# One block of window attention and routed experts on one core: v projected by 32x32 tiles beside q and k, router logits with tokens on the partitions

## The chip, the cores and the metric

The kernel runs on one core of one Trainium2 chip. The metric is the device time in microseconds (us), the median of the runs shown. TensorE is called PE, VectorE DVE, ScalarE ACT, GpSimd POOL and SyncE SP, as in the profile.

## What is computed

The input x is 8 images of 64 channels and 96 x 96 pixels, in fp32. A layer norm over the channels comes first, then attention in windows of 4 x 4 pixels, 8 heads, over each half of the channels, once plain and once rolled by two pixels, with a depthwise 3 x 3 convolution of v added. Then every pixel is a token for a mixture of 8 experts, of which the router picks two:

```python
qkv = jnp.einsum('oi,bihw->bohw', qkv_w, xh)
q, k, v = jnp.split(qkv, 3, axis=1)
lepe = jax.lax.conv_general_dilated(v, lepe_w, (1, 1), 'SAME', feature_group_count=c)
...
attn = jnp.einsum('nhqc,nhkc->nhqk', q * scale, k) + bias[None]
attn = jax.nn.softmax(attn, axis=-1)
out = jnp.einsum('nhqk,nhkc->nhqc', attn, v) + lepe
...
router_probs = jax.nn.softmax(x @ router_w + router_b, axis=-1)
top_p, top_i = jax.lax.top_k(router_probs, K)
expert_out = jnp.einsum('bnd,edc->bnec', x, expert_w) + expert_b
...
x = x + _L0_conv_ref(_ln_c(x), L0_conv_qkv_w, L0_conv_lepe_w, L0_conv_bias_table)
t = _to_tokens(x)
t = t + _L0_ffn_ref(_ln_t(t), L0_ffn_router_w, L0_ffn_router_b, L0_ffn_expert_w, L0_ffn_expert_b)
```

## The kernel before

Everything is one software pipeline, written out by hand. Its step is a **slot**: one unit of eight windows. Three units make a strip (4 image rows, 384 pixels) and two strips, six slots, make a tile. There are 576 units, 192 strips and 96 tiles. `LAG` says how many slots behind the start each stage works, and `pipeline()` calls every engine's `slot()` for each slot number: 72 slots written out, then a hardware loop of 72 slots (12 tiles, one image) that runs six times, then the rest written out. Each engine goes through its own instructions in the order of its `slot()`, and only semaphores tie the engines together, so an engine may be ahead of another by a slot or more. Below, "slot 0" to "slot 5" are slot numbers modulo six.

The channels and the plain and rolled copies fill the 128 partitions in four groups of 32. What PE does, by line of the kernel:

- every slot: **score** (L632, 32 matmuls of 32x32 with 64 columns, on top of a bias that ACT has placed in the bank) and **product** (L717, 32 matmuls with 32 columns of weights and 16 moving columns; in slots 1 and 4 also L723, the sums of the softmax, four matmuls into `bank_d`). In slots 2 and 5 the product begins a strip and waits for `fin_made` of the strip before, since both use `bank_o`.
- slots 2 and 5: **value** (L657), one 128x128 matmul with 384 columns. Slots 0 and 3: **q and k** (L670, L671), eight matmuls of 32x32 with 384 columns, each group of rows taking q to its own group of columns and k to the one two further on.
- by tile: **centre** (L731, slot 0), **variance** (L648, slot 1), the convolution in three steps (L697, slots 4, 5 and 0), **tile_sum** (L737, slot 3, needs `bank_p[1]` back from the k of the same slot), **tile_variance** (L742, slot 4), the expert bias (L756, slot 4), **turn_gates** (L640, slot 5), **router** (L748, slot 5), the turned logits (L681, slot 2), and the four expert pairs (L617), in slots 0, 1, 1 and 2.

The fp32 matmuls appear twice in the trace, as two passes of PE, so that the 32 matmuls of a score are 64 records.

ACT, in a slot: the softmax sums (L781, L783) after slots 1 and 4, v (L802), exp (L806), the bias for the score two units on (L812), q twice (L820), k (L829), and the norm's pieces (L841, L842 after tile_sum). DVE, in a slot: row maximum (L956) and subtraction (L961) of the last score, `y_out` (L970, needs the last expert pair), `fin` (L976, needs L783), the turned v (L984), `yn` (L995), the logits (L999), y in three steps (L991, L1005, L1011), the turned probabilities (L1019, needed by the product one slot later), and between them 17 small steps that choose the experts. POOL issues the DMAs that spread k and v (L573, L585) and pair `yn` (L595).

An expert pair's place in the slot is given by a table: place 0 is behind the score, place 1 behind q and k.

```python
EXPERT_AT = {(0, 0): 0, (1, 0): 1, (1, 1): 2, (2, 0): 3}
```

## Time and profile before

| | |
|---|---|
| median of 3 runs | 3418.93 us (3413.72 to 3419.05) |
| the profiled execution, its own time | 3416.38 us |
| its span, first to last instruction | 3414.6 us |
| busy: PE, DVE, ACT, POOL | 3076.2 us (90%), 2233.1 us (65%), 1619.7 us (47%), 2509.8 us (74%) |
| chain that ended last | PE 81%, issue 8%, DVE 5%, ACT 4% |
| granted PE clock, mean | 0.942 of full speed |
| instruction queue q8 | 688 packets, 11.27 MB |
| PE instructions | 84772 matmul records and as many weight loads |

A busy PE is not PE at its peak, since the ends of pipelined matmuls are modelled. What one group of matmuls costs is therefore read from its start to the start of the next group, not from its duration. The time in brackets behind a row is how long the engine stood idle ahead of it and for whom; "issue" is idle time in which it waited for nothing that the profile shows.

### The profile page before, as it was taken

The page shows a single profiled execution, that of the slowest core. Times are in us where ns is not written, and L with a number is a line of the kernel's source. Part 1 is how long each engine was busy: PE and PEld are TensorE (multiplying, and loading weights), DVE is VectorE, ACT ScalarE, POOL GpSimd, SP SyncE. Part 2 cuts the span into 40 slices and gives each one's busy share as a digit, 9 for nine tenths or more (in the row PEclk, how much of TensorE's full clock was granted, in tenths as well). Part 3 has the DMA queues.
Part 4 walks back from the last instruction along what each step waited for, and adds up shares of the span by engine and source line. Part 5 has one row for each costly group of instructions (what it writes and reads, how often), then busy time and mean ns, then how long its engine had stood idle before and what let it go on. Part 6 is the DMA issues. An engine that isn't in the chain of part 4 may idle for free.

```text
span 3414.6 us, 201082 instructions
## 1 busy us (share of the span) xinstructions
PE 3076.2 (90%) x84772; PEld 1798.8 (53%) x84772; DVE 2233.1 (65%) x4807; ACT 1619.7 (47%) x3362; POOL 2509.8 (74%) x4998
## 2 busy tenths in 40 slices
PE   4899999989989899998999989999899999999987
PEld 2555555545555455554555545555455555555553
DVE  2566767656666666666666757666666666666666
ACT  2554545445444454444444445444454444444441
POOL 4887777767777677777777767777677777777771
PEclk7999999999999999999999999999999999999998
DMA  2456665656565565556565656666565656565656
GB/s 64 105 138 160 159 160 155 160 131 168 148 167 149 145 165 147 155 153 153 150 168 147 163 139 158 161 155 166 133 170 148 168 152 163 152 162 146 163 138 178
DMA packets 436964, 517.64 MB, mean 152 GB/s; under 512 B 116400, under 2 KB 405168, under 8 KB 435888
## 3 DMA queue, kind: packets, MB, share of 16 engines
q1 hardware_dynamic: 270128, 390.67, 42.8%
q0 software_dynamic: 165888, 113.57, 13.9%
q8 instruction: 688, 11.27, 1.5%
q14 instruction: 260, 2.13, 0.2%
HBM read 312.67 MB, written 77.86 MB: 114 GB/s over the span
## 4 chain that ended last, share of the span: by engine, by line
PE 81%; issue 8%; DVE 5%; ACT 4%; DMA 1%; DVEq 0%; POOL 0%; SPq 0%; ACTq 0%; POOLq 0%
PE bank L632 18%; PE bank L717 14%; PE bank L697 13%; PE bank L617 9%; PE bank L723 4%; PE bank L657 3%; PE bank L670 3%; PE bank L737 3%; PE bank L742 2%; PE bank L731 2%; PE bank L756 2%; PE bank L648 2%; PE bank L748 2%; ACT qx L820 2%; ACT bank L812 1%
## 5 line engine op out<-in xcount | busy, mean ns | idle before, releaser
L585 POOL DMA_DIRECT2D vx<-vt x3072 | 1562.1, 517 | 443.6 <-PE bank L723 433.8
L573 POOL DMA_DIRECT2D kx<-k_sb x1536 | 739.2, 489 | 386.7 <-issue 241.7
L717 PEld LDWEIGHTS bank<-probT,vx 128*32 128x32 f32 x36864 | 605.5, 150 | 445.9 <-issue 387.8
L717 PE MATMUL bank<-probT,vx 128*32 128x16 f32 x36864 | 668.0, 210 | 146.9 <-issue 132.7
L632 PEld LDWEIGHTS bank<-kx,qx 32*32 32x32 f32 x36864 | 598.1, 112 | 345.4 <-issue 332.4
L632 PE MATMUL bank<-kx,qx 32*32 32x64 f32 x36864 | 700.7, 226 | 76.6 <-issue 54.2
L949 DVE TENSOR_TENSOR gx<-gate_wide,yn_pair 128x768 f32<-128x768 f32 x384 | 365.6, 953 | 384.5 <-PE bank L617 380.4
L697 PE MATMUL bank<-halo,conv_w 128*64 128x380 f32 (+6 forms) x2592 | 479.5, 497 | 0.1
L806 ACT ACTIVATE prob<-prob 128x512 f32<-128x512 f32 x576 | 360.0, 625 | 244.4 <-DVE prob L961 222.3
L961 DVE TENSOR_TENSOR prob<-bank,row_max 128x512 f32<-128x512 f32 x576 | 398.5, 692 | 16.7
L956 DVE TENSOR_REDUCE row_max<-bank 128x32 f32<-128x512 f32 x576 | 382.8, 665 | 37.8 <-PE bank L632 33.2
L1019 DVE STREAM_TRANSPOSE probT<-prob 128x512 f32<-128x512 f32 x576 | 405.1, 703 | 0.3
L976 DVE TENSOR_TENSOR fin<-bank,row_inv 128x384 f32<-128x384 f32 x192 | 106.2, 553 | 408.4 <-ACT row_inv L783 408.0
L617 PE MATMUL bank<-gx,table 128*64 128x384 f32 x1536 | 341.9, 525 | 5.8 <-DVE gx L949 4.2
L812 ACT ACTIVATE bank<-bias_tile 128x512 f32<-128x512 f32 x576 | 339.5, 589 | 0.0
L697 PEld LDWEIGHTS bank<-halo,conv_w 128*64 128x64 f32 x2592 | 180.9, 149 | 245.9 <-issue 236.7
L820 ACT ACTIVATE qx<-bank,table 128x384 f32<-128x384 f32 x384 | 200.6, 573 | 151.8 <-PE bank L670 151.7
L846 ACT ACTIVATE yrstd<-bank,table 128x384 f32<-128x384 f32 x96 | 55.8, 581 | 394.0 <-PE bank L742 394.0
L595 POOL DMA_DIRECT2D yn_pair<-yn x384 | 201.3, 531 | 51.4 <-DVE gx L949 33.8
L802 ACT ACTIVATE v_sb<-bank 128x384 f32<-128x384 f32 x192 | 94.4, 492 | 210.1 <-PE bank L657 209.6
L670 PE MATMUL bank<-xs,table 32*32 32x384 f32 x1536 | 180.1, 509 | 11.1 <-issue 9.8
L657 PE MATMUL bank<-xs,table 128*128 128x384 f32 x384 | 172.0, 530 | 19.6 <-DMA xs<-xn 19.6
(72 smaller groups left out, 2959.9 us busy)
## 6 DMA issues: line engine op xcount, KB each, us to landing
gate_wide<-gate_rows SPq DMA_DIRECT2D x768, 192.0 KB, 3.9
vx<-vt POOLq DMA_DIRECT2D x3072, 12.0 KB
halo<-xn SPq DMA_DIRECT2D x160, 240.0 KB
kx<-k_sb POOLq DMA_DIRECT2D x1536, 24.0 KB
z<-fin SPq DMA_DIRECT2D x192, 192.0 KB
yn_pair<-yn POOLq DMA_DIRECT2D x384, 96.0 KB, 3.2
xa<-in_x SPq DMA_DIRECT2D x96, 192.0 KB, 3.1
xn<-xa SPq DMA_DIRECT2D x192, 96.0 KB, 2.5
```

What stands on the lines that cost most here:

```text
L573: pool.dma_start(kx[to + m:to + C:4, r % 2, m, :], k_sb[at + m:at + C:4, r % 2, :])\
L585: pool.dma_start(vx[to:to + TOK, r % 2, col:col + 25:8, odd, :], vt[at:at + TOK, r % 2, x::2, :, :].rearrange("p h n k -> p h (n k)"))\
L617: last = MM(bank_f[half * C:(half + 1) * C, 0:SPX], const("experts")[:, p * C:(p + 1) * C], gx[:, p % 2, half, :], start=False, stop=(p == ...
L632: last = MM(bank_s[r % 2][at, w * KEYS:(w + 1) * KEYS], qx[at, kr % 2, win, :, :].rearrange("p a i -> p (a i)"), kx[at, kr % 2, :, win * T ...
L697: last = MM(by_rows(bank_c[half * C:(half + 1) * C, 0:SPX])[:, top:end, low:high], conv_w[:, which, group * 3 + side, :], by_rows(halo[:, ...
L717: last = MM(bank_o[32 * c:32 * c + 32, at * TOK:(at + 1) * TOK], vx[:, kr % 2, :, at % 2, at // 2 * 4 + ba], probT[:, kr % 2, at, ba * TOK ...
L806: S.activation(prob[:, r % 4, :], prob[:, r % 4, :], ACT.Exp).then_inc(exp_made, 1)
L812: S.activation(bank_s[r % 2][:, :], bias_tile[:, :, :].rearrange("p n k -> p (n k)"), ACT.Copy).then_inc(bias_placed, 1)
L949: V.tensor_tensor(gx[:, p % 2, :, :], gate_wide[:, p, :, :], yn_pair[:, r % 2, :, :], ALU.mult)\
L956: V.tensor_reduce(row_max[:, r % 2, :], per_row(bank_s[r % 2][:, :]), AX.X, ALU.max).then_inc(max_made, 1)
L961: V.tensor_tensor(per_row(prob[:, r % 4, :]), per_row(bank_s[r % 2][:, :]), over_keys(row_max[:, r % 2, :]), ALU.subtract).then_inc(shifte ...
L1019: V.transpose(probT[:, kr % 2, j * UW:(j + 1) * UW, :].rearrange("p n k -> p (n k)"), prob[:, r % 4, :]).then_inc(probT_made, 1)
```

## The change

Five things are done to the order and the shape of the work:

1. **v beside q and k.** The value matmul of slots 2 and 5 goes. In slots 0 and 3 each group of rows now makes three 32x32 matmuls, q to its own group of columns, v to the next and k to the one after; v goes to `bank_d`, the bank of the softmax sums, so the group waits for `log_made` and the sums wait for `v_copied`.
2. **Logits with tokens on the partitions.** The router's 128x16 matmul with 384 columns, ACT's copy of it (L852) and the three transposes in slot 2 (L681) go. Twelve matmuls with 32 tokens of `yn` as weights and the router's 16 columns moving take their place in slot 5; DVE adds the router's bias when it takes the logits, at the head of slot 0.
3. **Behind the product.** The convolution's steps of slots 5 and 0, and the expert pairs of place 1, stand behind the product; the last pair moves from slot 2 place 0 to slot 2 place 1.
4. **ACT** copies k first, then q twice, then v, all in slots 0 and 3.
5. **DVE** makes `y_out` at the end of slot 2 and no longer near its head.

```diff
-EXPERT_AT = {(0, 0): 0, (1, 0): 1, (1, 1): 2, (2, 0): 3}
+EXPERT_AT = {(0, 0): 0, (1, 0): 1, (1, 1): 2, (2, 1): 3}
...
                 if st := s.strip("query_key"):
                     k, r = st
                     if (s.n - LAG["router"] - 1) % TSLOT == 0 and (ti := Slot(s.n - 1, s.turn).tile("router")):
+                        pe.wait_ge(fln_made, ti[0] + 1)
+                        pe.wait_ge(logit_saved, ti[0] + 1)
+                    if s.later(r, 4):
+                        pe.wait_ge(log_made, k - 3)
...
+                    wait_alone(pe, xs_loaded[r // 2 % 2], (k // 4 + 1) * (XS_DMAS * 16))
                     for g in range(4):
+                        at, to_v, to_k = (slice((g + n) % 4 * CH, (g + n) % 4 * CH + CH) for n in range(3))
                         q_last = MM(bank_p[0][at, 0:SPX], wq[at, at], xs[at, r % 4, :], start=True, stop=True)
+                        k_last = MM(bank_p[1][to_k, 0:SPX], wk[at, at], xs[at, r % 4, :], start=True, stop=True)
+                        v_last = MM(bank_d[to_v, 0:SPX], wv[at, at], xs[at, r % 4, :], start=True, stop=True)
...
                     if j == UNITS - 1:
+                        pe.wait_ge(v_copied, strips_to(s, k + 4))
...
+                expert(1)
+                conv((1, 2))
...
-                    MM(bank_p[1][0:GE, 0:SPX], const("router"), yn[:, r % 2, :], start=True, stop=True)\
-                        .then_inc(logitT_made, 1)
+                    for blk in range(TBLK):
+                        for c in range(4):
+                            last = MM(bank_p[1][32 * c:32 * c + 32, blk * GE:(blk + 1) * GE],
+                                      yn[:, r % 2, blk * 128 + 32 * c:blk * 128 + 32 * c + 32], const("router"),
+                                      start=True, stop=True)
+                    last.then_inc(logit_made, 1)
```

On PE, from the variance of slot 1 to the product of slot 2, the order before was this (`gx` belongs to the expert pairs, `kx,qx` to the score, `probT,vx` to the product, `probT,table` to the softmax sums, `xs` to value, `logitT` to the turned logits):

```order
L648 MATMUL bank<-sq,table 128x384 [waits k_saved,sq_made]
...
L617 MATMUL bank<-gx,table 64x384 [waits gx_made]
L617 MATMUL bank<-gx,table 64x384
L717 MATMUL bank<-probT,vx 32x16 [waits probT_made]
L717 MATMUL bank<-probT,vx 32x16 x31
L723 MATMUL bank<-probT,table 32x384 x4
...
L632 MATMUL bank<-kx,qx 32x64 x31
...
L617 MATMUL bank<-gx,table 64x384
...
L657 MATMUL bank<-xs,table 128x384 [waits sq_made]
L681 MATMUL bank<-table,logitT 128x16 [waits ln_made,logitT_saved]
...
L717 MATMUL bank<-probT,vx 32x16 [waits log_made,fin_made,v_spread0]
```

And in the same place of the changed kernel (L672 is the variance, L707 the product, L714 the sums, L656 the score):

```order
L672 MATMUL bank<-sq,table 128x384 [waits k_saved,sq_made]
L707 MATMUL bank<-probT,vx 32x16 [waits probT_made]
L707 MATMUL bank<-probT,vx 32x16 x31
...
L714 MATMUL bank<-probT,table 32x384 [waits v_copied]
L714 MATMUL bank<-probT,table 32x384 x3
...
L617 MATMUL bank<-gx,table 64x384 [waits gx_made]
L617 MATMUL bank<-gx,table 64x384
...
L656 MATMUL bank<-kx,qx 32x64 x31
...
L707 MATMUL bank<-probT,vx 32x16 [waits log_made,fin_made,v_spread0]
```

The sums stand ahead of an expert pair, value and the turned logits are gone, and the product of slot 2 follows its score directly.

On ACT, slot 3 with what stands around it, before (from the placed bias of slot 2 to the norm after tile_sum):

```order
L812 ACTIVATE bank<-bias_tile 128x512 [waits shifted]
L806 ACTIVATE prob<-prob 128x512 [waits shifted]
L812 ACTIVATE bank<-bias_tile 128x512 [waits shifted]
L820 ACTIVATE qx<-bank,table 128x24x16 [waits q_made,score_made]
L820 ACTIVATE qx<-bank,table 128x24x16
L829 ACTIVATE k_sb<-bank 128x384 [waits k_spread1,k_made]
L841 ACTIVATE yn<-bank 128x384 [waits yn_paired1,fc_made]
```

The same place after the change:

```order
L803 ACTIVATE bank<-bias_tile 128x512 [waits shifted]
L797 ACTIVATE prob<-prob 128x512 [waits shifted]
L803 ACTIVATE bank<-bias_tile 128x512 [waits shifted]
L811 ACTIVATE k_sb<-bank 128x384 [waits k_spread1,k_made]
L819 ACTIVATE qx<-bank,table 128x24x16 [waits q_made,score_made]
L819 ACTIVATE qx<-bank,table 128x24x16
L827 ACTIVATE v_sb<-bank 128x384 [waits vt_made,v_made]
L838 ACTIVATE yn<-bank 128x384 [waits yn_paired1,fc_made]
```

The copy of k is now the first of four copies, and v the last.

On DVE, slot 2, before (with the row maximum of slot 2 at its head):

```order
L956 TENSOR_REDUCE row_max<-bank 128x32 [waits score_made]
L961 TENSOR_TENSOR prob<-bank,row_max 128x512 [waits max_made]
...
L970 TENSOR_TENSOR y_out<-bank,y 128x384 [waits out_stored1]
...
L976 TENSOR_TENSOR fin<-bank,row_inv 128x24x4x4 [waits z_stored1]
...
L1019 STREAM_TRANSPOSE probT<-prob 128x512 [waits exp_made]
```

And after, from the subtraction of slot 2 to the row maximum of slot 3:

```order
L958 TENSOR_TENSOR prob<-bank,row_max 128x512 [waits max_made]
...
L967 TENSOR_TENSOR fin<-bank,row_inv 128x24x4x4 [waits z_stored1]
...
L1006 STREAM_TRANSPOSE probT<-prob 128x512 [waits exp_made]
...
L1019 TENSOR_TENSOR y_out<-bank,y 128x384 [waits out_stored1]
...
L953 TENSOR_REDUCE row_max<-bank 128x32 [waits score_made]
```

`y_out` has gone from ahead of `fin` to behind the turned probabilities.

## Rows read from the trace of the kernel before

**Rows 1.** Windows, one turn of the loop: engines busy, PE clock, DMA share, GB/s.

```profile
1264.00:1684.00 420.00, 384.40 (x10564) 224.05 (x10564) 277.40 (x595) 200.81 (x417) 311.59 (x622) 0.94 0.59 153
```

**Rows 2.** Timeline of PE: start, us, line, operation, [idle before]; slot 1 to 3.

```profile
547.94 0.91 PE L648 MATMUL bank<-sq,table 128*128 128x384 f32 x2
548.78 0.87 PE L617 MATMUL bank<-gx,table 128*64 128x384 f32 x4
549.58 1.11 PE L717 MATMUL bank<-probT,vx 128*32 128x16 f32 x64
550.52 0.83 PE L723 MATMUL bank<-probT,table 128*32 128x384 f32 x8
551.28 1.10 PE L632 MATMUL bank<-kx,qx 32*32 32x64 f32 x64
...
553.10 0.91 PE L657 MATMUL bank<-xs,table 128*128 128x384 f32 x2
...
554.43 1.11 PE L717 MATMUL bank<-probT,vx 128*32 128x16 f32 x64
...
560.44 0.91 PE L737 MATMUL bank<-y,table 128*128 128x384 f32 x2 [1.82 <-ACT k_sb L829]
```

**Rows 3.** Timeline of ACT, slots 2 and 3 of the same tile.

```profile
551.42 0.49 ACT L781 ACTIVATE row_inv<-bank 128x384 f32<-128x384 f32 x1 [0.39 <-PE bank L723]
551.95 0.52 ACT L783 ACTIVATE row_inv<-row_inv 128x384 f32<-128x384 f32 x1
...
557.92 0.63 ACT L806 ACTIVATE prob<-prob 128x512 f32<-128x512 f32 x1 [2.36 <-DVE prob L961]
...
558.98 1.03 ACT L820 ACTIVATE qx<-bank,table 128x384 f32<-128x384 f32 x2
559.90 0.49 ACT L829 ACTIVATE k_sb<-bank 128x384 f32<-128x384 f32 x1
```

**Rows 4.** Timeline of DVE, slots 2 and 3 of the same tile.

```profile
553.31 0.56 DVE L970 TENSOR_TENSOR y_out<-bank,y 128x384 f32<-128x384 f32 x1 [1.36 <-PE bank L617]
...
557.19 0.69 DVE L961 TENSOR_TENSOR prob<-bank,row_max 128x512 f32<-128x512 f32 x1
```

**Rows 5.** Timeline of PE, slots 3 to 0 of the tile before.

```profile
526.88 1.33 PE L737 MATMUL bank<-y,table 128*128 128x384 f32 x2 [1.83 <-ACT k_sb L829]
...
533.46 0.91 PE L742 MATMUL bank<-ysq,table 128*128 128x384 f32 x2
...
536.32 0.82 PE L657 MATMUL bank<-xs,table 128*128 128x384 f32 x2
537.07 1.50 PE L697 MATMUL bank<-halo,conv_w 128*64 128x380 f32 x8
...
539.44 0.80 PE L748 MATMUL bank<-yn,table 128*16 128x384 f32 x2
540.17 1.09 PE L632 MATMUL bank<-kx,qx 32*32 32x64 f32 x64
541.20 0.87 PE L617 MATMUL bank<-gx,table 128*64 128x384 f32 x4
```

**Rows 6.** Timeline of PE, q and k of slot 0: first records of both passes, next group.

```profile
542.00 0.50 PE L670 MATMUL bank<-xs,table 32*32 32x384 f32 x1
...
542.34 0.48 PE L670 MATMUL bank<-xs,table 32*32 32x384 f32 x1
...
542.80 0.54 PE L697 MATMUL bank<-halo,conv_w 128*64 128x380 f32 x2
```

**Rows 7.** Timeline of DVE, `fin` of slot 5 in that tile.

```profile
536.60 0.56 DVE L976 TENSOR_TENSOR fin<-bank,row_inv 128x384 f32<-128x384 f32 x1 [4.19 <-ACT row_inv L783]
```

**Rows 8.** Waits of PE in 1180 to 1584: for whom, us, times, longest.

```profile
PE bank L717 <- issue: 15.6, 12, 2.0
```

**Rows 9.** Timeline of PE at the loop's branch, two turns.

```profile
1167.76 0.86 PE L632 MATMUL bank<-kx,qx 32*32 32x64 f32 x47 [3.28 <-issue]
...
1589.37 0.92 PE L632 MATMUL bank<-kx,qx 32*32 32x64 f32 x25 [3.02 <-issue]
```

More of the change, by code:

```diff
@@ L619, in expert, with conv @@
                     last.then_inc(expert_made, 1)
+                def conv(sides):
+                    ti = s.in_tile("conv")
+                    if not ti or ti[2] not in sides:
+                        return
+                    k, r, side = ti
+                    t, dw = (r + 1) % IMT, SIDES[side]
+                    if side == 0:
+                        pe.wait_ge(halo_loaded[r % 2], halos_to(s, r) * 16)
+                        if s.later(r, 1):
+                            pe.wait_ge(y_step, k * 2 - 1)
+                    low, high = max(0, -dw), W - max(0, dw)
+                    first = [side == 0, side == 0]
+                    for group, skip in ((0, 0), (1, 2)):
+                        parts = [(half, *rows) for half in range(2) for rows in conv_rows(t, half)[group]]
+                        for half, top, end, which in sorted(parts, key=lambda part: part[1]):
+                            at = half * SP + skip
+                            last = MM(by_rows(bank_c[half * C:(half + 1) * C, 0:SPX])[:, top:end, low:high],
+                                      conv_w[:, which, group * 3 + side, :],
+                                      by_rows(halo[:, r % 2, :])[:, at + top:at + end, low + dw:high + dw],
+                                      start=first[half], stop=(side == 2 and group == 1), skip_group_check=True)
+                            first[half] = False
+                    if side == 2:
+                        last.then_inc(conv_made, 1)
                 if u := s.unit("score"):
@@ L796, in slot @@
                     S.activation(rstd[:, r % 2, :], rstd[:, r % 2, :], ACT.Exp, scale=-0.5).then_inc(rstd_made, 1)
-                if st := s.strip("value"):
-                    k, r = st
-                    act.wait_ge(v_made, k + 1)
-                    if s.later(r, 2):
-                        act.wait_ge(vt_made, k - 1)
-                    S.activation(by_window(v_sb[:, r % 2, :]), windows(bank_p[0][:, 0:SPX]), ACT.Copy).then_inc(v_copied, 1)
                 if u := s.unit("shift"):
@@ L815, in slot @@
                     k, r = st
+                    act.wait_ge(k_made, k + 1)
+                    if s.later(r, 2):
+                        act.wait_ge(k_spread[r % 2], k // 2 * (K_DMAS * 16))
+                    S.activation(by_window(k_sb[:, r % 2, :]), windows(bank_p[1][:, 0:SPX]),
+                                 ACT.Copy).then_inc(k_saved, 1)
+                if st := s.strip("query_key"):
+                    k, r = st
                     if s.later(r, 2):
@@ L1026, in slot @@
                 gate_work((10, 12), (0, 0))
+                if yt := s.tile("tile_out"):
+                    k, r = yt
+                    dve.wait_ge(expert_made, (k + 1) * PAIRS)
+                    if s.later(r, 2):
+                        dve.wait_ge(out_stored[r % 2], k // 2 * 16)
+                    V.tensor_tensor(y_out[:, r % 2, :], bank_f[:, 0:SPX], y[:, r % 4, :], ALU.add).then_inc(y_out_made, 1)
             pipeline(dve, slot)
```

88 lines of the change are left out of this document (19 added, 69 removed).

## Prediction, made before the changed kernel ran

> **What bounds the kernel now.** I read the busy shares first, then the windows of one turn of the loop, and then the timelines of PE, ACT and DVE over one tile. In a turn PE is busy 384.40 of 420 us, against 277.40 for DVE, 200.81 for ACT and 311.59 for POOL [rows 1], so PE sets the pace and the question is what fills its 35 us per tile (the loop's branch comes again after 1589.37 - 1167.76 = 421.6 us, which is 12 tiles) [rows 9]. The reader is to see two kinds of stretch. From the variance of slot 1 to the tile_sum of slot 3, 547.94 to 560.44, PE takes 12.50 us and stands idle 1.82 us at the end, waiting for ACT's copy of k [rows 2]. That copy is the end of a chain that starts on PE itself: expert pair, `y_out`, then DVE without a pause to the subtraction of slot 3 (553.31 to 557.88), then ACT: exp, bias, q twice, k [rows 3, 4]. From tile_sum to the next variance (526.88 to 547.94, 21.06 us) PE has no wait and is the bound by itself [rows 2, 5].
>
> Two losses lie on top. The clock granted over the turn is 0.94, which with levels of 2.4 and 1.2 GHz means 12% of the time at 1.2 GHz, so 6% of 35 us, 2.1 us a tile. And PE waits for "issue" inside the product: 15.6 us in 12 waits over 12 tiles, 1.3 us a tile [rows 1, 8].
>
> **The change, part by part.** All of it is summed against the profiled execution, span 3414.6 and time 3416.4 us; the median of the runs is 2.5 us above that, which I leave out.
>
> *Value, slot 5.* Its 128x128 matmul goes: 537.07 - 536.32 = 0.75 us from start to start [rows 5]. *Value and turned logits, slot 2:* 554.43 - 553.10 = 1.33 us [rows 2]. *v beside q and k.* q and k, sixteen records, take 542.80 - 542.00 = 0.80 us, of which the two passes are 0.34 us apart and the eight records of a pass start within 0.04 us [rows 6]. No row shows three groups of rows writing into one group of columns. The bounds: 0.03 us if four more tiles start beside the others (two passes of four records at that spacing), 0.68 us (two passes of 0.34) if v goes in passes of its own, and up to 8 x 0.34 = 2.7 us if its tiles queue one behind another. I take 0.03, since the nearest row, the softmax sums, has four matmuls stream different data through the same rows at once: eight records of 384 columns in 551.28 - 550.52 = 0.76 us, where one after another at 0.34 us they would take 2.7 us [rows 2, 6]. Below nothing is excluded, since work is only added there.
>
> That the four q tiles, which lie in different groups of rows and share one PSUM bank, start together is what the same sixteen records show. The Trainium skill (TensorEngine Tiling, Gotcha 1: PSUM Pressure) says the opposite, that different row tiles cannot use the same bank at the same time; by that rule q and k would take 2.7 us or more, and v would add as much again. The trace does not agree at 0.80 us, so the rule stays a rival only.
>
> *Router, slot 5.* The old matmul takes 540.17 - 539.44 = 0.73 us [rows 5]. The new one is 24 records of the product's form, whose 64 take 550.52 - 549.58 = 0.94 us [rows 2]: 24/64 of it, 0.35 us. Bounds: 0.2 (a quarter of the product's time) and 0.73 as before. Saved: 0.38 us. ACT loses a copy, which was never late; DVE's logits become an addition of the same size.
>
> *Moves of the expert pairs and the convolution.* They change nothing in PE's sum. What they change is who waits. The products of slots 2 and 5 wait for `fin`, and now come sooner after what `fin` depends on.
>
> *Slot 5.* `fin` starts 536.60 - 533.46 = 3.14 us after tile_variance and lasts 0.56 [rows 5, 7]; nothing in the change makes it earlier. The product would come where value stood, 536.32 - 533.46 = 2.86 us after it. It starts at 3.14 + 0.56 + 0.1 = 3.8: a **new wait** of 0.95 us, where the old order had value and the convolution in front. Behind the waiting product stand the convolution, the router and the next score; all slip by it. The bounds are nothing and 1.4 us (if v_copied or the turned v holds DVE up).
>
> *Slots 1 to 3.* Count from the variance, 0. The sums come ahead of an expert pair (0.80 us, 549.58 - 548.78 [rows 2]), but ACT is busy until its 0.39 us of idle time [rows 3], so L783 ends 552.47 - 0.39 = 552.08, at 4.14, and `fin` runs from 4.2 to 4.75. PE reaches the product of slot 2 at 0.84 + 0.94 + 0.76 + 0.80 + 1.03 = 4.37 (a score is 541.20 - 540.17 = 1.03 [rows 2, 5]) and waits 0.4 us. `y_out` no longer stands first and waits for nobody; DVE's run from `y_out` to the end of the subtraction was 557.88 - 553.31 = 4.57 us [rows 4] and holds the same operations in another order, less 0.1 us for the logits. So the subtraction of slot 3 ends at 4.2 + 4.5 = 8.7. ACT adds exp and bias, 558.98 - 557.92 = 1.06 us, and then k, 0.49 us, where q twice (559.90 - 558.98 = 0.92 us) used to come between [rows 3]. k is there at 10.3. PE by itself is done at 4.8 + 0.94 + 0.80 + 1.03 + 0.83 + 0.94 = 9.35 and waits about 0.95 us. tile_sum starts at 10.3 where it started at 12.50: 2.2 us saved.
>
> *Tile_sum to variance:* - 0.75 - 0.38 + 0.95 + 0.03 = 0.15 us saved.
>
> *Queues.* ACT's copy of v in slots 0 and 3 is last of four and delays the norm's copies after tile_sum by some 0.4 us; tile_variance comes three groups later (over 3 us), which covers it. DVE now takes the logits at the head of slot 0, so its slot 0 cannot start before PE's router is done; behind that wait stand the row maximum and two products for the experts, which PE needs only after its own score and expert pair of slot 0 (1.83 us) or later. POOL has the same DMAs; at 311.59 busy of a shorter 385 us it is at 81%, not the bound. `y_out` is stored about 1.5 us later and SP's loads of the next strips behind it are due three slots on. These I cost at nothing; if POOL's cover were gone, the spread of v would hold the product of slots 2 and 5.
>
> **Sum.** 2.2 + 0.15 = 2.35 us a tile, times 96 = 226 us: 3416 - 226 = 3190. Then the losses on top. PE's idle time at the end of slot 3 falls from 1.8 to about 0.95 us, and the slow clock stands behind that idle time; if a third of the 2.1 us goes, 0.7 us a tile comes back. Against it, the issue waits were partly hidden under the wait for k and are now barer: I give back 0.5 us. Net 0.2 us a tile, 20 us. **Forecast: 3170 us**, 7% faster, by itself 3085 to 3255 (the ends are the losses 0.9 us a tile better or worse).
>
> **The rivals.**
>
> *The clock stays up.* With idle stretches halved, the falls behind slot 3 vanish: 1.5 of the 2.1 us a tile come back instead of 0.7, and the issue waits cost nothing more: 1.3 x 96 = 125 us less, 3045 to 3065. For it: the slow stretch follows the 1.83 us wait (a tile_sum of 1.33 us there against 0.91 [rows 2, 5]). Against it: new waits in slots 2 and 5.
>
> *v in passes of its own:* 0.65 x 192 = 125 us more, 3295. For it: nothing was seen with three groups of rows into one of columns. Against it: the sums' row above.
>
> *Instruction supply.* A matmul is four records with its weight loads. A tile has six more for v (24 records) and, for the router, 48 new records less 4 and less the 6 of the three transposes: 62 more on (84772 x 2)/96 = 1766, 3.5%, and slots 2 to 4 are packed tighter. The issue waits (1.3 us a tile [rows 8]) are the sign of it. If they double in a stretch that used to be padded by waits, 1.3 - 0.5 = 0.8 us a tile, 77 us, and the clock stays as it is, 67 more: 3315. The Trainium skill (Advanced Engine Details and Errata, ISA Cache) states that instructions come in lines of 256; then a tile is 7 lines before and 7.1 after, and the positions of the waits would drift.
>
> *Slower: the tiles of v queue.* If each of v's eight passes has to follow another in its bank or its columns, the group grows by 2.7 us, 192 x 2.7 = 518 us: 3190 + 518 = 3710. It decides from 226/192 = 1.2 us a strip on. For it is the rule of the skill above; against it are q and k and the sums.
>
> *No change:* the wait for `fin` in both slots is so long that the gain is gone (over 2.35 us more a tile). It would need `fin` 2 us later than rows 7 put it.
>
> **How the numbers follow.** Forecast 0.66; clock stays up 0.08; v in passes of its own 0.09; instruction supply 0.11; v queues 0.04; no change 0.02. The likeliest is 3170. The range 3060 to 3300 holds the forecast, the clock case in part, and v in its own passes, and leaves out some 2 in 10: the tails and the slower cases. A measurement of this kernel can tell about 0.2% from no change. Faster by over 0.2%: 0.94; within: 0.02; slower: 0.04.
>
> **What would show it.** In the profile after, q, k and v: 24 records that start within 0.5 us, next group 0.8 to 0.9 us after the first. The product of slot 5 with about 0.9 us of idle time for `fin`, that of slot 2 with 0.4. tile_sum 10.3 us behind the variance, with about 1 us of idle time for k, and 19 to 21 us from there to the next variance. A router of 24 records in under 0.5 us. A granted clock over 0.95. I would be wrong if the group of q, k and v takes over 1.5 us, if the wait for k at tile_sum is still 1.8 us, or if "issue" grows to over 3 us a tile.

## The result, and the profile after

The changed kernel takes 3379.01 us (median of 12 runs, 3361.2 to 3398.93), the kernel before 3413.59 us on the same chips (12 runs). The ratio is 0.9909, 95% interval 0.9884 to 0.9935: 0.9% faster, where 7% was forecast, and outside the stated range. The profiled run took 3377.19 us, its span is 3374.9 us, its granted clock 0.958 (0.942 before).

First one of the two shortest full tiles of the changed kernel (30.5 us each), in the timeline of PE. It is called the **clean** tile below, since little is late in it. (Columns as in [rows 2]; L672 is the variance, L707 the product, L714 the sums, L656 the score, L730 tile_sum, L735 tile_variance.)

```profile
1499.59 0.91 PE L735 MATMUL bank<-ysq,table 128*128 128x384 f32 x2
...
1503.39 1.14 PE L707 MATMUL bank<-probT,vx 128*32 128x16 f32 x64 [0.78 <-issue]
1504.47 1.50 PE L637 MATMUL bank<-halo,conv_w 128*64 128x380 f32 x8
1505.89 0.38 PE L743 MATMUL bank<-table,yn 128*32 128x16 f32 x24
1506.21 0.86 PE L656 MATMUL bank<-kx,qx 32*32 32x64 f32 x47
1507.54 0.43 PE L656 MATMUL bank<-kx,qx 32*32 32x64 f32 x17 [0.47 <-issue]
...
1514.66 0.91 PE L672 MATMUL bank<-sq,table 128*128 128x384 f32 x2
1515.51 1.11 PE L707 MATMUL bank<-probT,vx 128*32 128x16 f32 x64
1516.45 0.82 PE L714 MATMUL bank<-probT,table 128*32 128x384 f32 x8
1517.20 0.87 PE L617 MATMUL bank<-gx,table 128*64 128x384 f32 x4
1518.00 1.09 PE L656 MATMUL bank<-kx,qx 32*32 32x64 f32 x64
1519.51 1.12 PE L707 MATMUL bank<-probT,vx 128*32 128x16 f32 x64 [0.41 <-issue]
...
1522.52 0.48 PE L687 MATMUL bank<-xs,table 32*32 32x384 f32 x1
...
1523.35 0.42 PE L707 MATMUL bank<-probT,vx 128*32 128x16 f32 x14
1524.06 0.93 PE L707 MATMUL bank<-probT,vx 128*32 128x16 f32 x50 [0.29 <-issue]
1525.05 0.91 PE L730 MATMUL bank<-y,table 128*128 128x384 f32 x2
...
1530.07 0.91 PE L735 MATMUL bank<-ysq,table 128*128 128x384 f32 x2
```

Most steps of the prediction are here to be read. q, k and v go from 1522.52 to the product at 1523.35, 0.83 us, against 0.80 for q and k alone [rows 6]. The new router takes 1506.21 - 1505.89 = 0.32 us. The waits for `fin` are 0.78 us in slot 5 and 0.41 us in slot 2 (the view calls them issue; they end 0.10 to 0.15 us after `fin` does). Variance to tile_sum is 10.39 us, where it was 12.50 [rows 2]. The whole tile, from tile_variance to tile_variance, is 30.48 us at a granted clock of 1.00; the tile of the prediction's rows took 560.44 - 526.88 = 33.56 us at 0.95 [rows 2, 5]. DVE and ACT end the chain to k as worked out, and tile_sum follows k at once (1525.05). But the wait for k that was to stand there, 0.95 us, is not to be seen: 0.29 us of issue inside the product ahead of tile_sum have taken part of its place.

```profile
1518.85 0.56 DVE L967 TENSOR_TENSOR fin<-bank,row_inv 128x384 f32<-128x384 f32 x1 [0.18 <-ACT row_inv L780]
...
1522.75 0.69 DVE L958 TENSOR_TENSOR prob<-bank,row_max 128x512 f32<-128x512 f32 x1
```

```profile
1523.47 0.63 ACT L797 ACTIVATE prob<-prob 128x512 f32<-128x512 f32 x1 [3.65 <-DVE prob L958]
...
1524.53 0.47 ACT L811 ACTIVATE k_sb<-bank 128x384 f32<-128x384 f32 x1
```

But such a tile is rare. The mean from tile to tile is 34.2 us in the changed kernel and 34.6 us before, loop branches included. The gain of a clean tile is 3.1 us, a part of it the clock, and all but some 0.4 us of it is gone in the mean. The waits of PE over the whole execution (for whom, us in total, times, longest) show where:

```profile
PE bank L707 <- issue: 177.7, 247, 2.3
PE bank L656 <- issue: 125.2, 127, 5.4
PE bank L707 <- DVE fin L967: 35.9, 52, 1.9
...
PE bank L637 <- issue: 12.6, 16, 2.0
PE bank L743 <- issue: 12.2, 12, 2.2
```

The same view of before:

```profile
PE bank L717 <- issue: 132.7, 92, 3.0
PE bank L632 <- issue: 54.2, 42, 3.9
PE bank L737 <- ACT k_sb L829: 46.9, 51, 1.8
```

All issue rows together are 366 us after and 199 us before. Waits for `fin` explain little of it. In the changed kernel 138 of the 192 products of slots 2 and 5 start 0.10 to 0.15 us after a `fin` ended, most after a wait of about 0.4 or 0.7 us. That is 76.5 us in all, of which some 41 us stand in the issue rows. The other 325 us stand for "waits for nothing that the profile shows". They are in scores of slots 0 and 3, in the router, in q, k and v, in the convolution: not behind any one operation. What they have in common is a count. From one such wait to the next, in this stretch of the changed kernel:

```profile
1119.07 0.46 PE L656 MATMUL bank<-kx,qx 32*32 32x64 f32 x17 [1.13 <-issue]
1119.47 0.29 PE L664 MATMUL bank<-table,gate_tmp 128*48 128x128 f32 x1
1119.69 1.11 PE L707 MATMUL bank<-probT,vx 128*32 128x16 f32 x64
1120.73 1.50 PE L637 MATMUL bank<-halo,conv_w 128*64 128x380 f32 x8
1122.16 0.38 PE L743 MATMUL bank<-table,yn 128*32 128x16 f32 x24
1122.47 0.41 PE L656 MATMUL bank<-kx,qx 32*32 32x64 f32 x11
1123.82 0.87 PE L656 MATMUL bank<-kx,qx 32*32 32x64 f32 x48 [0.94 <-issue]
```

17 + 1 + 64 + 8 + 24 + 11 = 125 matmul records, each with a weight load, are 250 instructions, and the trace has 6 register and semaphore instructions of PE between them: 256. They come 4.75 us after the last such wait. Counting every record of PE from the start of the execution, waits of this stretch fall at one remainder of 256:

```
time of the wait        844.51  854.83  877.90  892.64  972.44  995.55  1013.88  1076.17  1105.41  1123.82
instructions mod 256       140     139     140     139     139     140      139      139      140      140
```

Up to the loop's first branch and in every turn of the loop the same holds, each time with another remainder (193, 139, 85, 31, 233, 179). In the kernel before, the issue waits of 1.4 us and more between 874 and 1151 us fall at 174 or 175, while the waits for k at 945.4, 979.0 and 1013.3 us fall at 143, 156 and 168. PE's instructions come in pieces of 256, and at these points the next piece is not there. The Trainium skill (Advanced Engine Details and Errata, ISA Cache) gives 256 instructions as the size of a cache line; the trace agrees.

The trace also has the transfers that bring the pieces, in the instruction queue q8: packets of 16384 bytes. Their number goes with PE's instructions: 688 before, 711 after, and 567 in e_half below, which has 384 x 96 = 36864 = 144 x 256 instructions fewer than the changed kernel.

```profile
q8 instruction: 711, 11.65, 1.6%
```

```profile
q8 instruction: 567, 9.29, 1.4%
```

Call a wait of over 0.3 us at the remainder of its turn, give or take one, a **late piece** (the first 256 instructions behind a branch are left out). The changed kernel has 287, and 286 of them end 1.1 to 1.9 us after such a packet has landed; of its other waits of over 0.3 us that is so for 3 in 63. In the kernel before it is so for all 113, and for 10 in 89 others. From the begin of one piece to that of a late one, exactly one packet starts, in 286 cases of 287. By the medians it starts 1.8 us after PE has begun the piece before, takes 1.2 us, and PE goes on 1.4 us after it has landed: 4.4 us from piece to piece, with nine tenths of the cases between 3.7 and 6.0. Late pieces are 263 us in the changed kernel and 162 us in the one before.

With this the profiled executions balance. PE's busy time falls by 3076.2 - 2897.0 = 179 us. Its idle time rises by 139 us: late pieces 101 more, `fin` 76 more, k 43 less, and 5 us of others. The span falls by the 40 us that are left.

```profile
PE 2897.0 (86%) x87748; PEld 1745.2 (52%) x87748; DVE 2245.1 (67%) x4807; ACT 1549.9 (46%) x3266; POOL 2509.6 (74%) x4998
```

### The profile page after: what moved, and what is told of

Read it like the earlier page. It is cut to its first block, busy times and chain, and to the rows that moved or that the text cites. A ratio compares the mean times of both kernels' runs of the same rounds, so it can differ in the third digit from the quotient of the medians.

```text
span 3374.9 us, 206835 instructions
## 1 busy us (share of the span) xinstructions
PE 2897.0 (86%) x87748; PEld 1745.2 (52%) x87748; DVE 2245.1 (67%) x4807; ACT 1549.9 (46%) x3266; POOL 2509.6 (74%) x4998
## 2 busy tenths in 40 slices
DMA packets 436986, 518.03 MB, mean 153 GB/s; under 512 B 116400, under 2 KB 405168, under 8 KB 435888
## 4 chain that ended last, share of the span: by engine, by line
PE 78%; issue 13%; ACT 4%; DVE 2%; DMA 1%; SPq 1%; ACTq 0%; DVEq 0%
PE bank L707 18%; PE bank L656 17%; PE bank L637 13%; PE bank L617 8%; PE bank L687 4%; PE bank L714 3%; PE bank L730 3%; PE bank L724 2%; PE bank L672 2%; PE bank L735 2%; PE bank L753 2%; PE bank L688 1%; PE bank L743 1%; ACT row_inv L780 1%; DVE fin L967 1%
## 5 line engine op out<-in xcount | busy, mean ns | idle before, releaser
L707 PEld LDWEIGHTS bank<-probT,vx 128*32 128x32 f32 x36864 | 617.2, 150 | 499.6 <-issue 471.4
L707 PE MATMUL bank<-probT,vx 128*32 128x16 f32 x36864 | 682.1, 210 | 215.6 <-issue 177.7
L656 PE MATMUL bank<-kx,qx 32*32 32x64 f32 x36864 | 701.5, 222 | 131.6 <-issue 125.2
L656 PEld LDWEIGHTS bank<-kx,qx 32*32 32x32 f32 x36864 | 586.9, 109 | 397.8 <-issue 382.4
L637 PE MATMUL bank<-halo,conv_w 128*64 128x380 f32 (+6 forms) x2592 | 464.4, 477 | 12.9 <-issue 12.6
L617 PE MATMUL bank<-gx,table 128*64 128x384 f32 x1536 | 350.3, 531 | 15.5 <-issue 9.4
L637 PEld LDWEIGHTS bank<-halo,conv_w 128*64 128x64 f32 x2592 | 169.2, 140 | 140.2 <-issue 121.4
L687 PE MATMUL bank<-xs,table 32*32 32x384 f32 x1536 | 192.1, 525 | 29.1 <-DMA xs<-xn 19.0
L689 PE MATMUL bank<-xs,table 32*32 32x384 f32 x1536 | 196.8, 527 | 7.7 <-issue 7.7
L688 PE MATMUL bank<-xs,table 32*32 32x384 f32 x1536 | 191.5, 527 | 11.1 <-issue 11.1
```

What stands on the lines that cost most here:

```text
L617: last = MM(bank_f[half * C:(half + 1) * C, 0:SPX], const("experts")[:, p * C:(p + 1) * C], gx[:, p % 2, half, :], start=False, stop=(p == ...
L637: last = MM(by_rows(bank_c[half * C:(half + 1) * C, 0:SPX])[:, top:end, low:high], conv_w[:, which, group * 3 + side, :], by_rows(halo[:, ...
L656: last = MM(bank_s[r % 2][at, w * KEYS:(w + 1) * KEYS], qx[at, kr % 2, win, :, :].rearrange("p a i -> p (a i)"), kx[at, kr % 2, :, win * T ...
L707: last = MM(bank_o[32 * c:32 * c + 32, at * TOK:(at + 1) * TOK], vx[:, kr % 2, :, at % 2, at // 2 * 4 + ba], probT[:, kr % 2, at, ba * TOK ...
```

## The experiments

Ratios are to the kernel before, run beside each kernel on the same chip. "Instructions a tile" are all records of PE in the trace, divided by 96. (The texts written ahead of the runs leave out most of the register and semaphore instructions: their 1779, 1805, 1817 and 1841 are 26 to 28 too low, and the differences stay.) "Late pieces" are counted as above. Profiles are of one execution each.

| kernel | instructions a tile | ratio (95%) | issue rows, us | late pieces, us | clock |
|---|---|---|---|---|---|
| before | 1807 | 1 | 199 | 162 | 0.942 |
| changed | 1868 | 0.991 (0.988 to 0.994) | 366 | 263 | 0.958 |
| e_fill | 1868 | 0.993 (0.991 to 0.996) | 381 | 360 | 0.939 |
| e_narrow | 1868 | 0.987 (0.983 to 0.992) | 452 | 370 | 0.926 |
| e_light | 1868 | 0.961 (0.958 to 0.963) | 293 | 187 | 0.974 |
| e_half | 1484 | 0.871 (0.869 to 0.873) | 215 | 90 | 0.972 |
| e_half_before | 1423 | 0.923 (0.919 to 0.928) | 76 | 59 | 0.956 |
| e_half_k | 1423 | 0.904 (0.900 to 0.907) | 37 | 9 | 0.964 |
| e_kfirst_yout | 1807 | 0.975 (0.973 to 0.978) | 192 | 151 | 0.968 |
| e_kfirst | 1807 | 0.992 (0.989 to 0.995) | 219 | 186 | 0.957 |
| e_yout | 1807 | 1.001 (0.999 to 1.004) | 149 | 119 | 0.949 |
| e_light_k | 1807 | 0.947 (0.945 to 0.950) | 113 | 82 | 0.978 |
| e_k_router3 | 1809 | 0.977 (0.974 to 0.981) | 200 | 164 | 0.967 |
| e_k_v | 1832 | 0.980 (0.976 to 0.984) | 298 | 248 | 0.939 |
| e_router3 | 1832 | 0.990 (0.987 to 0.993) | 347 | 233 | 0.956 |
| e_k_router | 1845 | 0.983 (0.977 to 0.989) | 243 | 204 | 0.962 |
| e_vwhole | 1844 | 0.995 (0.992 to 0.998) | 295 | 187 | 0.963 |
| e_places | 1868 | 0.989 (0.986 to 0.993) | 356 | 329 | 0.941 |

### Two theories

The **waits theory** says that PE's work and the waits in its order set the time, so that work taken away or a wait covered comes back in full. The **supply theory** says that the next 256 instructions take 4 to 5 us to arrive, so that a tile of 1868 instructions (7.3 pieces) has a bound of its own. The time of a piece is no constant: the clean tile got its 7.3 in 30.48 us, 4.2 us each.

**e_fill** covers the waits for `fin`.

```diff
-EXPERT_AT = {(0, 0): 0, (1, 0): 1, (1, 1): 2, (2, 1): 3}
+EXPERT_AT = {(0, 0): 0, (1, 0): 1, (1, 1): 2, (2, 0): 3}
-                conv((0,))
+                conv((0, 1))
...
-                conv((1, 2))
+                conv((2,))
```

> The changed kernel with the convolution's step of slot 5 and the last expert pair put back ahead of the product, so that PE has work while it waits for fin (0.92 and 0.52 us of idle time a tile). Waits theory (PE's own work and the waits in its order set the time, and issue waits only add to them): the 1.4 us a tile come back, 138 us, about 3240 us. Supply theory (the next 256 instructions of PE take 4 to 5 us to arrive, and a tile of 1840 instructions is 7.2 such pieces, so that a tile cannot go much below 33 us): the idle time for fin goes and issue takes its place, 3330 to 3360 us.

3392.8 us, ratio 0.9934: nothing came back. Both theories had expected a gain, the supply theory 3330 to 3360 us.

```profile
PE bank L656 <- issue: 151.7, 127, 4.1
PE bank L707 <- issue: 132.9, 140, 2.3
PE bank L688 <- issue: 25.9, 20, 1.9
```

The row for `fin` falls from 35.9 to 4.9 us (8 times), and 107 of the 247 issue waits ahead of the product are gone. Waits ahead of the score, of q, k, v and of the router grew: late pieces are 97 us more, where the waits for `fin` had been 76.5 us. Those waits, which looked like the obvious loss (the text above put them at 138 us), were not what the time hung on.

**e_narrow** takes 2 us a tile of work from PE and no instruction.

```diff
-                    low, high = max(0, -dw), W - max(0, dw)
+                    low, high = max(0, -dw), W // 2 - max(0, dw)
```

> The changed kernel with every matmul of the convolution over half the columns (the right half of each image row is left out; as many instructions as before). PE's own work falls by 3 x 0.7 = 2.0 us a tile, its instruction count not at all. Waits theory: 195 us less, 3185 us. Supply theory: at most a third of it, 3310 us or more, with issue waits up by over 1 us a tile.

3368.05 us: 0.4% less than the changed kernel, with intervals that overlap, where the work removed was put at 195 us. (In the profile the convolution's own busy time falls from 464 to 278 us, 186 less.)

```profile
PE 2788.1 (83%) x87750; PEld 1772.0 (53%) x87750; DVE 2245.7 (67%) x4807; ACT 1551.1 (46%) x3266; POOL 2509.5 (75%) x4998
```

```profile
PE bank L708 <- issue: 201.6, 260, 2.9
PE bank L657 <- issue: 139.3, 128, 4.6
PE bank L744 <- issue: 28.9, 20, 2.9
```

PE is busy 109 us less than in the changed kernel (2897.0), and its late pieces are 107 us more. The clock is 0.926, down from 0.958, and the other matmuls take longer: that is where the 77 us between 186 and 109 went. So of 186 us about four tenths went to the clock and most of the rest to waiting.

**e_half** takes 384 instructions a tile away and about as much work as e_narrow (the product's columns stay, in half as many matmuls).

```diff
-                    for w in range(UW):
+                    for w in range(0, UW, 2):
...
-                            last = MM(bank_o[32 * c:32 * c + 32, at * TOK:(at + 1) * TOK],
+                            last = MM(bank_o[32 * c:32 * c + 32, at * TOK:(at + 2) * TOK],
-                                      probT[:, kr % 2, at, ba * TOK:(ba + 1) * TOK], start=True, stop=True)
+                                      probT[:, kr % 2, at:at + 2, ba * TOK:(ba + 1) * TOK], start=True, stop=True)
```

> The changed kernel with the product in 16 matmuls of 32 moving columns where it has 32 of 16 (the columns streamed are as many; windows with odd numbers are taken with the wrong weights). PE has 384 of its 1840 instructions a tile less, and at most 6 x 0.45 = 2.7 us less work. Waits theory: at most 260 us less, 3120 us. Supply theory: a tile is 5.7 pieces of 256 instructions and no longer limited by them, so the issue waits (beside those for fin) nearly vanish and the work alone is left, 30.5 - 2.7 = 27.8 us a tile, 2850 to 2950 us.

2972.32 us, 407 us less. From e_narrow and e_half together it follows that it is instructions, not work, that PE is short of: 2 us of work a tile are worth 11 us in all, and 2.7 us of work with 384 instructions are worth 407. The 2.7 us by themselves could be worth 260 at most. Late pieces fall from 263 to 90 us, and the clock rises to 0.972, which has its share in the 407. The gain is more than the waits theory allows, and the time is 22 us above the supply theory's range: the issue waits did not quite vanish (215 us; waits for `fin` are 93 us in all), and the wait for k has come back as the next bound:

```profile
PE bank L707 <- issue: 131.6, 190, 2.9
PE bank L730 <- ACT k_sb L811: 59.1, 71, 1.8
```

**e_light** leaves PE as it is and takes a quarter of the DMA traffic away (518.03 to 385.91 MB). The columns that are no longer written are set to 0 once, at the start.

```diff
-                        sp.dma_start(gate_wide[odd * C:(odd + 1) * C, p, :, :],
-                                     by_expert[odd, p].unsqueeze(0).broadcast_to([C, 2, SPX]))\
+                        sp.dma_start(gate_wide[odd * C:(odd + 1) * C, p, :, 0:SPX // 8],
+                                     by_expert[odd, p][:, 0:SPX // 8].unsqueeze(0).broadcast_to([C, 2, SPX // 8]))\
```

> The changed kernel with the spread of the gates cut to an eighth of its columns (the other gates stay 0): same DMAs in number, 129 MB less of 518. Supply theory, if it is the other DMA traffic that makes the instructions late: issue waits fall by half or more, 3230 to 3290 us. Supply theory, if the arrival does not depend on traffic: 3370 us. Waits theory: within 20 us of 3379.

3272.11 us, 107 us less. In before and after PE's waits for the gated input (`DVE gx`) are 4.2 and 5.9 us in all, so the traffic costs time in another way.

```profile
PE bank L709 <- issue: 155.1, 226, 1.8
PE bank L658 <- issue: 99.5, 112, 5.1
PE bank L709 <- DVE fin L969: 39.7, 57, 1.9
```

The issue rows fall from 366 to 293 us, and late pieces from 263 to 187 us: by three tenths, not by half as I expected, though the time lies in the range. The direction is that of the supply theory: from the begin of a piece to a late next one it is 4.2 us in the median, 4.4 in the changed kernel, and the packet itself takes 1.14 us instead of 1.20. About half of the gain is in PE's busy time (2836.0 us, 61 less) at a clock of 0.974. That the clock rises because PE waits less often fits, but was not shown by itself; neither was how the queues share the engines.

### Is the change worth its work where instructions are not short?

**e_half_before** is the kernel before with the edit of e_half.

> The kernel before with the product in 16 matmuls of 32 moving columns where it has 32 of 16 (odd windows taken with wrong weights), as in the run of the changed kernel with the same edit, 2972 us. It asks what the change is worth where the supply of instructions is no longer short. Supply theory: the whole sum of the prediction comes out, 2.35 us a tile, so the kernel before takes 2972 + 226 = 3200 us, 3150 to 3220. Waits theory (the sum of work itself was wrong): the change is worth some 35 us here as there, 3000 to 3030 us.

3165.73 us, ratio 0.9232, against 0.8712 for the changed kernel with the same edit: 5.2 points, 0.052 x 3412 = 177 us. The sum had said 226. With late pieces down to 59 and 90 us the prediction's steps are worth four fifths of what they were put at; with instructions short, a seventh. In this kernel the wait that the prediction counted on is large, and issue is small:

```profile
PE bank L737 <- ACT k_sb L829: 173.9, 85, 2.4
PE bank L632 <- ACT bank L812: 94.0, 192, 2.3
PE bank L632 <- issue: 40.1, 17, 3.7
```

### Fewer instructions in the changed kernel

**e_router3** makes the router's logits in three matmuls of 128 tokens.

```diff
-                        for c in range(4):
-                            last = MM(bank_p[1][32 * c:32 * c + 32, blk * GE:(blk + 1) * GE],
-                                      yn[:, r % 2, blk * 128 + 32 * c:blk * 128 + 32 * c + 32], const("router"),
-                                      start=True, stop=True)
+                        last = MM(bank_p[1][:, blk * GE:(blk + 1) * GE],
+                                  yn[:, r % 2, blk * 128:(blk + 1) * 128], const("router"), start=True, stop=True)
```

> The changed kernel with the router in three matmuls of 128 tokens by 16 columns where it has twelve of 32 tokens: 36 instructions a tile less (1841 to 1805), some 0.5 us a tile more of PE's own work, since its weight loads are four times as wide. Supply theory: 36/256 of 4.7 us is 0.66 us a tile, 63 us less, part of it given back to PE's work: 3320 to 3365 us. Waits theory: 48 us more, 3425 us.

3389.65 us beside a kernel before at 3431.9, ratio 0.9897: no different from the changed kernel. It decides little: neither the loss of the waits theory (1.4%) nor the gain that the supply theory had put at 14 us or more.

**e_vwhole** takes v by one 128x128 matmul behind q and k.

```diff
-                        v_last = MM(bank_d[to_v, 0:SPX], wv[at, at], xs[at, r % 4, :], start=True, stop=True)
...
-                    v_last.then_inc(v_made, 1)
+                    MM(bank_d[:, 0:SPX], wv, xs[:, r % 4, :], start=True, stop=True).then_inc(v_made, 1)
```

> The changed kernel with v by one 128x128 matmul right behind the tiles of q and k, and the spread of v from the old partitions: 24 instructions a tile less (1841 to 1817), 2 x 0.8 = 1.6 us a tile more of PE's own work. Waits theory: 154 us more, 3530 us. Supply theory: 24/256 of 4.7 us is 0.44 us a tile, 42 us less, and PE's work, hidden behind the waits for instructions for the most part, gives some of it back: 3345 to 3400 us.

3411.68 us, ratio 0.9949. Against the changed kernel that is 0.4% more, 14 us, where PE has 154 us more work. Nine tenths of that work disappear: late pieces are 76 us less (187 for 263), and PE's busy time is 125 us more, not 154.

### Which part carries the gain

**e_kfirst_yout** is the kernel before with only two of the five edits: ACT copies k before q, and `y_out` goes to the end of DVE's slot 2.

> The kernel before with only two things of the change: ACT copies k ahead of q, and DVE makes y_out at the end of slot 2. PE's instructions are those of the kernel before. The wait of tile_sum for k (47 us in all) should go in either theory. Waits theory: that is 47 us or more off, 3360 us or less. Supply theory: issue waits take its place, 3385 to 3412 us.

3339.18 us, ratio 0.9752 (0.9725 to 0.978): more than the whole change gives. This is outside what the supply theory had expected (3385 or more), and PE's instructions are the same.

```profile
PE bank L717 <- issue: 84.8, 95, 2.0
PE bank L632 <- issue: 80.7, 64, 4.7
...
PE bank L737 <- ACT k_sb L820: 18.8, 20, 1.1
```

The wait for k falls from 46.9 to 18.8 us, only 28 us, and the span by 80. Late pieces stay nearly as they were (151 us for 162). Most of the gain is in PE's busy time, 3016.7 us against 3076.2 for the same instructions: 59.5 us. The granted clock, 0.968 against 0.942, would account for up to 83 us of it (3076 x (1 - 0.942/0.968), an estimate); the two profiles are of different chips. In the kernel before, the clock fell to 0.54 in the stretch right behind the wait for k:

```profile
527.00:530.00 3.00, 3.00 (x66) 1.87 (x66) 2.22 (x7) 1.64 (x5) 1.06 (x3) 0.54 1.00 232
```

**e_kfirst** and **e_yout** make the two edits one at a time.

> The kernel before with ACT copying k ahead of q and nothing else. PE's wait for k ends 0.92 us sooner. If k's copy carries the gain: ratio 0.978 to 0.985. If y_out carries it: 0.990 to 0.997.

> The kernel before with y_out at the end of DVE's slot 2 and nothing else. DVE no longer stands 1.36 us for the last expert pair at the head of the chain to k, but has the same work behind fin, which starts some 1.1 us earlier. If y_out carries the gain: ratio 0.978 to 0.985. If k's copy carries it: 0.990 to 0.997.

3371.52 us, ratio 0.9917 (0.9885 to 0.9949) for k first; 3403.64 us, 1.0013 (0.9991 to 1.0035) for `y_out` alone. Neither lies where its text had put it (0.978 to 0.985 for the part that carries the gain, 0.990 to 0.997 for the other). The two alone add up to 0.7% and together give 2.5%. Their profiles show what a wait taken away uncovers. With k first, the wait for k is 15.8 us and late pieces are 186 us, 31 less and 24 more than before. With `y_out` late, the wait for k is 87.4 us (91 times, where it was 51) and late pieces are 119 us, 41 more and 43 less. Together they leave 18.8 and 151 us. Why the pair gives more than its sum was not taken apart further; PE's busy time (35 and 13 us less, together 60) goes the same way.

```profile
PE bank L737 <- ACT k_sb L829: 87.4, 91, 2.1
```

**e_k_v**, **e_k_router**, **e_k_router3** add one more part to e_kfirst_yout: v by tiles, the router in twelve matmuls, the router in three. **e_places** is the changed kernel without its third edit: expert pairs and convolution all ahead of the product.

> The kernel with k first and y_out late (ratio 0.975 to the kernel before), and in addition v by 32x32 tiles beside q and k; router, expert pairs and convolution as before. 24 instructions a tile more (1779 to 1803), 1.5 us a tile less work for PE. Work theory: 145 us less than without v, ratio 0.933. Supply theory (a tile takes at least 4.7 us for every 256 instructions): 24 instructions are 0.44 us a tile, 42 us more, ratio 0.98 to 0.99.

> The kernel with k first and y_out late, and in addition the router's logits with tokens on the partitions in twelve matmuls; v, expert pairs and convolution as before. 38 instructions a tile more (1779 to 1817), 0.73 + 0.49 - 0.32 = 0.9 us a tile less work for PE. Work theory: 86 us less, ratio 0.950. Supply theory: 0.7 us a tile more, 67 us, ratio 0.985 to 0.995.

> As the run before it, with the router in three matmuls of 128 tokens by 16 columns: 1781 instructions a tile, as many as the kernel with k first and y_out late (1779). PE's work falls by some 0.5 us a tile. Work theory: 45 us less, ratio 0.962. Supply theory: no change, ratio 0.970 to 0.978; and it should beat the form with twelve matmuls, by 30 to 60 us, though it is more work for PE.

> The changed kernel with all expert pairs and all three steps of the convolution at their old places, ahead of the product (v by tiles, logits by tokens, k first, y_out late stay). Work theory: the waits for fin are covered and 1.4 us a tile come back, ratio 0.950. Supply theory: 1841 instructions a tile as in the changed kernel, ratio 0.990, 0.985 to 0.995.

3336.49 us (0.9797), 3352.7 us (0.983), 3331.02 us (0.9774) and 3373.32 us (0.9892). v by tiles saves 1.5 us a tile of work and does not make the kernel faster than 0.975; neither does either router. Late pieces go from 151 us to 248 with v, to 204 with the router in twelve and to 164 with the router in three. The form with three matmuls has the lower median of the two though it is more work, 22 us less where 30 to 60 had been expected, and their intervals overlap. And the third edit is worth nothing either way (0.9892 against 0.9909). By number of instructions, these kernels stand in order: 1807, 1809, 1832, 1845 and 1868 instructions a tile have 0.975, 0.977, 0.980, 0.983 and 0.989 to 0.991, though neighbours in this row have intervals that overlap. The last step is larger than the 23 instructions in it explain, so the parts together lose something more; that was not isolated.

**e_half_k** and **e_light_k** make the edits of e_half and e_light in e_kfirst_yout.

> The kernel with k first and y_out late, with the product in 16 matmuls of 32 columns where it has 32 of 16 (odd windows taken with wrong weights): instructions are not short. Supply theory: here v by tiles, the router by tokens and the places are worth what PE's work says, so this kernel lies well between before (0.923) and changed (0.871) with the same edit: 0.895 to 0.910. If the rest of the change were worth nothing in itself, it would be at 0.871 to 0.88.

> The kernel with k first and y_out late, with the spread of the gates cut to an eighth of its columns (129 MB less traffic, the other gates 0). PE's instructions and work are unchanged. Supply theory: the same change of traffic gave the changed kernel 0.961 for 0.991, three points; here the instructions are fewer and the work is more, so one to two points: 0.955 to 0.965. If traffic does not matter where instructions are fewer: 0.970 or more.

3073.23 us (0.9036, 0.9004 to 0.9067) and 3221.4 us (0.9474). So where the product's instructions are halved, the change goes from 0.923 (before) over 0.904 (k first, `y_out` late) to 0.871 (all). The last step, 3.2 points or some 110 us, is v, router and places: the parts that gave nothing, or a loss of 1.6 points, at full instruction count. The issue rows of e_half_k are down to 37 us in all, its late pieces to 9. And 132 MB less traffic (517.64 to 385.52) gave 2.8 points, as much as in the changed kernel (3.0) and more than I had put it at. Late pieces fall from 151 to 82 us, so the supply takes its part of the better kernel's time too.

## Why the prediction was wrong

**Right:** the costs read from rows. q, k and v 0.83 us (0.83 forecast), router 0.32 (0.35), the waits for `fin` 0.41 and 0.78 us in the clean tile (0.4 and 0.95), variance to tile_sum 10.39 (10.3), DVE and ACT on the chain to k, the clock above 0.95. Three groups of rows do write into one group of columns at once. The Trainium skill's rule against several row tiles in one PSUM bank (TensorEngine Tiling, Gotcha 1: PSUM Pressure) found no support in twelve tiles that take 0.83 us.

**Wrong:** the step that put the losses on top of the sum: "the issue waits were partly hidden under the wait for k and are now barer: I give back 0.5 us", after they had been read as 1.3 us a tile. It sized them as a remainder, where they had a cause that the change makes worse, 61 instructions a tile more in less time. Late pieces were 162 us before and are 263 us after: 1.1 us a tile more in place of 0.5. The changed kernel's issue rows are 366/96 = 3.8 us a tile, which is over the 3 us that the prediction had named as the sign of being wrong.

The second part of the error is the wait for k. The sum took it from one tile as 1.82 us in every tile and took 0.95 us as what is left, 0.87 us a tile or 84 us to be won. Over the whole execution it was 46.9 us, in 51 tiles, and fell to 4.3. In the other tiles of the kernel before, PE waited for instructions instead, and then little or not at all for k: taking the one wait away could uncover only the other, as e_kfirst and e_yout show in both directions. That 10.39 us in the clean tile agrees with 10.3 is right for the chain to k; PE itself was to arrive 0.95 us earlier and did not.

Sum and clean tile were right, 31.2 us by the sum and 30.48 measured at full clock; the mean stayed at 34.2 us, of which 2.7 are late pieces. The rows could have raised the question: 35.1 us a tile in the kernel before [rows 9] are 5.0 us for each of its 7.1 pieces, a tile of 33.56 us is 4.75. They do not give the limit, but the work that was to remain, about 31 us with 61 instructions more, needed a piece every 4.3 us, and whether that could be supplied was not asked. A late piece comes after 4.4 us in the median.

**The rival** "instruction supply" named the mechanism and had a chance of 0.11; its price, 3315 us, was too low by 64. Its own term was near: 1.3 us a tile were to double, and late pieces went from 1.7 to 2.7 us. What it lacked is the other side: the sum it stood on had counted waits for k that most tiles did not have, and work that could not be won back while the next piece was missing. As point of decision it should have had the one shown by e_narrow: from there on, less work is worth nothing.

**The range** took the losses as 0.9 us a tile better or worse. They were 2.2 us a tile worse.

**Two things in one:** the prediction gave all five edits one sum. Two of them, k first and `y_out`, remove a wait, add no instruction, and are worth 2.5%, most of it by the clock. The other three trade work for instructions or for other waits, and take 1.6 points of that away.

The best kernel run is e_kfirst_yout, 0.975; e_k_router3, e_k_v are the same within their intervals.

## What to carry to other kernels

Before work is taken off the busiest engine, count its instructions in the stretch and divide: if "issue" waits recur at a fixed count of instructions (here 256), the supply of instructions is a bound, and the edit to look for is the one with fewer, larger instructions. Half as many matmuls for the product, over the same columns, gave 12% here (e_half, which takes the odd windows with other windows' weights); that more work for fewer instructions pays was not shown (e_router3 and e_vwhole gained nothing). A wait in the order is worth removing when it costs no instruction. Packing a 128x128 matmul into 32x32 tiles makes four times as many of them, and each 256 of them are another piece to wait for.

## What the runs showed of the hardware

- PE's instructions came in pieces of 256, one packet of 16384 bytes each on queue q8. With one exception in 287, a wait at the border of two pieces ended 1.1 to 1.9 us after such a packet had landed. The packet of a late piece started 1.8 us after PE had begun the piece before (median), so that late pieces followed 4.4 us after it (3.7 to 6.0). The shortest tile ran at 4.2 us a piece. With a quarter less DMA traffic the kernels were 2.8 to 3.0 points faster with the same instructions, and late pieces fell from 263 to 187 and from 151 to 82 us.
- Twelve 32x32 matmuls of 384 columns, three to each group of rows and of columns, into three PSUM banks, took 0.83 us, 0.03 us more than eight.
- Work taken from a PE that was short of instructions went with a lower granted clock: 0.958 to 0.926 for 2 us a tile less work (e_narrow).
- A kernel whose waits of up to 1.8 us for k were taken away (e_kfirst_yout) had a granted clock of 0.968 for 0.942, and PE was busy 59.5 us less with the same instructions.
